# Where four table rows are summed: VectorE or accumulating transfers, in one stage of a two-layer macaron kernel

## The reference, cut to what matters

```python
x = x + 0.5 * _L0_ffn_ref(_layernorm(x), ...)   # 32 routed experts, top 4, plus a shared one
x = x + _L0_attn_ref(_layernorm(x), ...)        # gated linear attention
x = x + 0.5 * _L0_ffn_ref(_layernorm(x), ...)   # the routed experts again
x = x + 0.5 * _L1_ffn_ref(_layernorm(x), ...)   # 8 experts, top 2   <- the stage of the change
x = x + _L1_attn_ref(_layernorm(x), ...)        # token mixing with a scan
x = x + 0.5 * _L1_ffn_ref(_layernorm(x), ...)
```

## Time and profile before

| what | value |
|---|---|
| runs shown | 1115.69, 1108.85 and 1122.56 us, median 1115.69 |
| profiled execution | 1114.38 us, of which the span of the trace is 1112.5 us |
| granted TensorE clock, mean of the span | 0.94 |
| busy share of the span | TensorE 88%, VectorE 65%, ScalarE 50%, GpSimd 34% |
| stage ffn1a | 744.3 us (mark L1962) to 871.3 us, when the token mixing starts |
| stage ffn1b | 1015.4 us (mark) to 1112 us |

### The profile page before, as it was taken

One profiled execution on the slowest core, in us unless ns is written; L12 is line 12 of the kernel. 1 busy time (PEld: TensorE's weight loads), 2 busy tenths in 40 slices (PEclk: granted clock), 3 DMA queues, 4 the chain that ended last, 5 costly groups with the idle time before them and its releaser, 6 DMA issues. The chain is left out here.

```text
span 1112.5 us, 17325 instructions
## 1 busy us (share of the span) xinstructions
PE 980.2 (88%) x5222; PEld 602.2 (54%) x5240; DVE 720.9 (65%) x2533; ACT 551.0 (50%) x1066; POOL 378.6 (34%) x452
## 2 busy tenths in 40 slices
PE   6999699979999799998999898956778899994886
PEld 4756566645565366665756666532334466553442
DVE  4588333137885467665688533159987699974885
ACT  6621233325666645547722333326667555534893
POOL 3106767820000223323105777801111156531110
PEclk9999799998999699999999999987889899996998
DMA  9859978864440802004246888757420000000012
GB/s 326 322 179 316 161 201 228 156 171 152 152 151 0 319 32 95 38 38 143 79 160 123 188 199 189 134 185 240 152 75 1 1 0 1 0 1 0 21 57 76
DMA packets 79656, 140.73 MB, mean 126 GB/s; under 512 B 16304, under 2 KB 47392, under 8 KB 77472
## 3 DMA queue, kind: packets, MB, share of 16 engines
q1 hardware_dynamic: 64224, 117.57, 30.8%
q0 software_dynamic: 15360, 22.29, 13.3%
HBM read 82.17 MB, written 58.72 MB: 127 GB/s over the span
## 5 line engine op out<-in xcount | busy, mean ns | idle before, releaser
L737 POOL DMA_INDIRECT ffn_sums<-ffn0a_xT,ffn0a_into x40 | 62.7, 1567 | 19.9 <-issue 9.3
L737 POOL DMA_INDIRECT ffn_sums<-ffn0b_xT,ffn0b_into x40 | 62.6, 1564 | 14.7 <-issue 9.5
L2291 PE MATMUL main_ps_k<-dense_first_xb,main_w 128*128 128x512 bf16 x112 | 37.8, 410 | 17.5 <-ACT ffn1a_silu L2226 8.3
L2716 PE MATMUL main_ps_k<-mixing_first_xk,mixing_wk 128*128 128x512 f32 (+1 forms) x96 | 47.0, 613 | 4.2 <-POOL main_opened_mark L1962 4.2
L1768 POOL TENSOR_TENSOR attn_attend_state_m<-attn_attend_state,attn_attend_heads 128x512 f32<-128x512 f32 x15 | 19.1, 1274 | 88.4 <-DVE attn_attend_state L1811 82.9
L2721 PE MATMUL attn_ps_r<-mixing_first_xr,mixing_wr 128*128 128x512 f32 (+1 forms) x96 | 46.2, 605 | 0.0
L1193 DVE TENSOR_TENSOR ffn0b_h<-ffn0b_sg,ffn0b_ps_b 128x160 f32<-128x160 f32 x32 | 10.3, 321 | 54.9 <-ACT ffn0b_sg L1028 54.8
L1193 DVE TENSOR_TENSOR ffn0a_h<-ffn0a_sg,ffn0a_ps_b 128x160 f32<-128x160 f32 x32 | 10.3, 321 | 54.2 <-ACT ffn0a_sg L1028 54.1
L2731 PE MATMUL attn_ps_y<-mixing_wv,attn_out 128*128 128x256 f32 (+1 forms) x192 | 43.0, 379 | 1.2 <-ACT attn_yn L2673 1.2
L866 PE MATMUL ffn0b_ps_b<-ffn0b_early,main_x 128*128 128x160 f32 x256 | 41.3, 305 | 2.6 <-DMA main_x<-w_experts 2.3
L888 PE MATMUL ffn0a_ps_b<-main_x,ffn0a_h 128*32 128x256 f32 (+2 forms) x144 | 43.5, 403 | 0.0
(11 more groups left out here) (498 smaller groups left out, 2682.3 us busy)
## 6 DMA issues: line engine op xcount, KB each, us to landing
main_spare<-ffn_sums SPq DMA_DIRECT2D x28, 1024.0 KB, 5.4
main_x<-w_experts SPq DMA_DIRECT2D x16, 1536.0 KB, 7.0
ffn_sums<-main_lent SPq DMA_DIRECT2D x36, 512.0 KB, 6.0
ffn_sums<-main_x SPq DMA_DIRECT2D x28, 512.0 KB, 4.1
ffn_rows<-ffn0a_early SPq DMA_DIRECT2D x8, 512.0 KB, 9.3
main_spare<-ffn_sums SPq DMA_DIRECT2D x8, 512.0 KB, 4.7
ffn_rows<-ffn0b_early SPq DMA_DIRECT2D x8, 512.0 KB, 2.9
x_out<-main_x SPq DMA_DIRECT2D x8, 512.0 KB, 2.9
```

What stands on the lines that cost most here:

```text
L737: g.indirect_dma_start(out=sums[:, :], out_offset=IndirectOffsetOnAxis(ap=into[:, at, j:j + 1], axis=0), in_=ys[:, n % NY, :], in_offset=N ...
L2291: ins = mm(ps[:], wt[:, k, m * P:(m + 1) * P], xb[:, p, k, :], start=k == 0, stop=k == KD - 1)
L2716: ins = mm(ps_k[0:rows, m % 2], wk[:, k, at:at + rows], xk[:, p, k, :], start=k == 0, stop=k == KD - 1)
```

## The change

For blocks 4 to 7 VectorE no longer adds rows. SyncE loads table 0's rows of a block (512 KB) straight into x (`sp_base`); GpSimd then issues three transfers of 512 KB for each block, which add the rows of tables 1, 2 and 3 to x (`pool_sum`), each when the one before has landed in the same block. VectorE waits for the last of them (`dve_summed`) and takes the moments. Blocks 1 to 3 are summed as before.

```diff
+    def sp_base(self, b):
+        tiles = slice(b * BT, (b + 1) * BT)
+        self.nc.sync.dma_start(self.x[:, tiles, :], self.by_row[:, 0, tiles]).then_inc(self.base_landed[b - 4], 16)
+
+    def pool_sum(self, b, n):
+        g, tiles = self.nc.gpsimd, slice(b * BT, (b + 1) * BT)
+        if n == 1:
+            g.wait_ge(self.base_landed[b - 4], 16)
+        else:
+            g.wait_ge(self.part_summed[b - 4], 16 * (n - 1))
+        if n == NTAB - 1 and b >= 6:
+            g.wait_ge(self.x_summed[b % 2], 16 * (b // 2 - 2))
+        ins = g.dma_start(self.x[:, tiles, :], self.by_row[:, n, tiles], accum_op=ALU.add)
...
+    def dve_summed(self, j):
+        (b, p, i), v = j, self.nc.vector
+        v.wait_ge(self.x_summed[p], 16 * i - 16)
+        v.memset(self.waiter[:], 0.0)
...
                 if combine:
-                    for b in range(2, NB):
-                        combine.sp(b)
-                        if b == 3 and load_next:
-                            load_next()
+                    combine.sp(2)
+                    for b in range(4, 7):
+                        combine.sp_base(b)
+                    sp.wait_ge(xb_made, 1)
+                    combine.sp_base(7)
+                    combine.sp(3)
+                    if load_next:
+                        load_next()
...
-                each(pool, ln.pool, NB, 1 if combine else 2)
+                if combine:
+                    ln.pool(number(1))
+                    combine.pool_sum(4, 1)
+                    combine.pool_sum(5, 1)
+                    ln.pool(number(2))
+                    combine.pool_sum(4, 2)
+                    combine.pool_sum(5, 2)
+                    combine.pool_sum(6, 1)
+                    ln.pool(number(3))
+                    combine.pool_sum(4, 3)
+                    combine.pool_sum(5, 3)
+                    combine.pool_sum(6, 2)
+                    combine.pool_sum(7, 1)
+                    ln.pool(number(4))
+                    combine.pool_sum(6, 3)
+                    combine.pool_sum(7, 2)
+                    ln.pool(number(5))
+                    combine.pool_sum(7, 3)
+                    ln.pool(number(6))
+                    ln.pool(number(7))
...
-                        if m == 0 and j2 and combine:
+                        whole = combine and j2 and isinstance(j2[0], int)
+                        if m == 0 and whole:
                             combine.dve(j2, 0)
                         if m == 2 and j2:
-                            if combine:
+                            if whole:
                                 combine.dve(j2, 1)
+                            elif combine:
+                                combine.dve_summed(j2)
                             moments(j2)
```

More of the change, by code:

```diff
@@ L1316, in __init__, with into_x @@
         self.late_step = sc.sem(f"{name}_late_step")
+    def into_x(self, sc):
+        self.base_landed = [sc.sem(f"base_landed{b}") for b in range(4, NB)]
+        self.part_summed = [sc.sem(f"part_summed{b}") for b in range(4, NB)]
+        self.x_summed = [sc.sem(f"x_summed{p}") for p in range(2)]
+    def sp_base(self, b):
[10 more added lines that the diff above has]
+        ins = g.dma_start(self.x[:, tiles, :], self.by_row[:, n, tiles], accum_op=ALU.add)
+        if n < NTAB - 1:
+            ins.then_inc(self.part_summed[b - 4], 16)
+        else:
+            ins.then_inc(self.x_summed[b % 2], 16)
+    def dve_summed(self, j):
+        (b, p, i), v = j, self.nc.vector
+        v.wait_ge(self.x_summed[p], 16 * i - 16)
+        v.memset(self.waiter[:], 0.0)
     def sp_first(self, n):
@@ L2070, in ffn1 @@
         G_STEPS = 10
+        if combine:
+            combine.into_x(sc)
         def tile_of(j):
@@ L2093, in _ @@
                 opened.pool()
-                each(pool, ln.pool, NB, 1 if combine else 2)
+                if combine:
+                    ln.pool(number(1))
[17 more added lines that the diff above has]
+                    ln.pool(number(7))
+                else:
+                    each(pool, ln.pool, NB, 2)
                 if following:
```

## The result

With the change the kernel takes 1104.13 us (median of 17 runs, 1101.23 to 1109.07), against 1115.69 us for the kernel before (17 runs). The ratio is 0.9901, with a 95% interval of 0.9882 to 0.9919: faster by 1%, some 11 us. The forecast was 1108, the range 1097 to 1119. The profiled execution took 1103.4 us, with a span of 1101.5 us. It starts the stage at 747.08 us (before 744.26) and the token mixing at 860.23 us (before 871.21).

A forecast was written before the change was run, and what follows sets the result against it. VectorE was taken to bound rounds 2 to 5 of ffn1a (busy 51.2 of 54.6 us). 1114.4 - 14.0 (additions removed) + 5.0 (block 3) + 2.5 (block 4 and TensorE's clock) = 1107.9, stated as 1108; range 1097 to 1119.

The forecast's parts named there:

- What is removed: Rounds 2 to 5 of ffn1a: without VectorE's additions they shorten from 54.6 to ffn1b's 40.6 us, at most 14.0 us gained.
- Block 3: VectorE's first addition of block 3 waits for its load behind four 0.5 MB loads and beside sums: 5.0 us, ends 1.0 and 7.6.
- the 210 of the experts' weights: Block 3's half beside sums: load rate of 210 GB/s, from 1.5 MB in 7.5 us beside scattering additions; wait 4.8 us.
- The upper end: Wait at block 3 if its half shares the DMA engines equally with the first sums of blocks 4 and 5: 7.6 us.
- Block 4 and TensorE's clock: Rounds 2 to 5: wait for block 4's last sum and TensorE's lower clock, together 2.5 us, ends 0 and 6.6.
- The price of a sum: DMA engines' time for a 0.52 MB sum at the scattering additions' 144 GB/s: 3.6 us of all engines.
- the 1 to 2 us of GpSimd's time: On GpSimd: each of the 12 transfers should take 1 to 2 us to issue.
- The landing of 7.2 us: Block 4's third sum: lands 4.5 us plus 2.7 us after its issue, at 783.1 us.
- a sign of being wrong: Prediction is wrong if sums land later than 10 us after issue, block 3's wait is gone, or rounds do not shorten.
- rounds 6 to 9 do not change: Last four rounds of ffn1a: they hold no sum and do not change.
- All of it arrives: Rival: loads go at 350 GB/s, sums land in time, block 3 waits 1.0 us; 1101.4 us, chance 0.20.
- Given back inside the stage: Rival: block 3 waits 7.6 us and TensorE keeps today's clock in rounds 2 to 5 (6.6 us); 1114.6 us, chance 0.20.
- Slower: Rival: the twelve sums come one behind the other, 7.5 us each, block 7 ready at 849; 1137 us, chance 0.07.

The follow-up runs named there:

- the two pairs of profiles: Changed kernel and kernel before, each profiled once, then each run once more without any edit for a second profile: 1106.26 us and 1114.1 us.
- the one with the busier TensorE: Kernel before, with the first matmul of each of TensorE's eight group-opening products per round done twice in rounds 2 to 5 of ffn1a: 1116.59 us.
- both moves: Changed kernel, loads of blocks 6 and 7 behind block 3's, first sums of blocks 4 and 5 behind block 2's `ln.pool`, block 3's `ln.pool` moved ahead: 1108.76 us.
- plain copies: Changed kernel with GpSimd's twelve transfers as plain copies that overwrite x instead of adding to it: 1104.4 us, ratio 0.9905.
- the second and third experiments: Changed kernel, second: loads of blocks 6 and 7 behind block 3's halves, 1100.58 us; third: first sums of blocks 4 and 5 behind block 2's `ln.pool`, 1100.9 us.

## Why the prediction was right, and where it was not

**What is removed: right.** 14.0 us were forecast for rounds 2 to 5; the two pairs of profiles show 13.9 and 14.1. The argument, that ffn1b is the same code without the sums and so shows the floor, gave the length of these rounds to 0.1 us (40.6 and 40.7), and the additions put back on VectorE take it away again.

**Block 3: right in size, through two errors that cancel.** 5.0 us were forecast, with ends of 1.0 and 7.6; the waits are 4.62 and 3.74 us, the opening is longer by 4.7 and 3.1. Loads and sums sharing the engines was the assumed cause, and either taken away removes the wait. But they did not share as the sum has it. Here are the two DMA queues of the changed kernel, q1 with SyncE's loads and q0 with GpSimd's sums (packets, MB, share of all engines), first from 757.1 to 764.1 us, where q0 has moved almost nothing although the first sum was issued at 760.01, then from 764.1 to 771.1:

```profile
q1 hardware_dynamic: 977, 2.85, 102.7%
q0 software_dynamic: 1, 0.00, 0.5%
```

```profile
q0 software_dynamic: 284, 1.04, 75.0%
q1 hardware_dynamic: 362, 0.71, 30.1%
```

In the first stretch the loads go at 407 GB/s, where the sum took 269. By its end SyncE's queue has moved 5.00 MB since the stage opened; the loads up to and with block 3's first half are 5.24 MB. In the second the loads get 101 GB/s, where the sum took the 210 of the experts' weights beside scattering additions, and the half lands only at 771.2, when the first sum and nearly all of the second are done. Faster loads up to the sums and slower ones beside them came to about the forecast wait: that the size is right is luck. The upper end stood for an equal share of the DMA engines between the two queues. The Trainium skill ("DMA: Bandwidth & Descriptors", section Queues, rings and completion order) says that an engine takes its queues in turn, packet by packet. The trace is in keeping with that, 284 packets against 362, but not with equal time: one of a sum took 0.30 us of an engine on average and one of a load 0.09 (share x 7 us x 16 engines / packets).

**Block 4 and TensorE's clock: mis-sized.** 2.5 us were put down for both, and measured is nothing: the memset has no wait, and TensorE has 0.98 in rounds 2 to 5. The sum itself came as forecast: issued 36.3 us behind the mark (783.41 - 747.08; forecast 775.82 + 5.0 - 744.26 = 36.6) and landed 5.5 us later, at 788.9, where the sum had 7.2 (it makes 783.1 of 775.82 + 7.2, which is 783.0). VectorE got there at 789.85. It is a narrow escape: with the loads in the other order the same memset waits 0.60 us. The price of a sum was well bounded: 144 GB/s were assumed, 160 measured alone; the 1 to 2 us of GpSimd's time came out at 0.9. The landing of 7.2 us lies between the 5.6 alone and the 8.2 in company. Three of the twelve landed later than 10 us after their issue (10.7, 11.4 and 11.5), which the prediction had named as a sign of being wrong; VectorE waited for none of them. The Trainium skill's fit for a transfer that GpSimd issues ("DMA: Bandwidth & Descriptors", Anatomy of one DMA: about 2.0 us plus the bytes at 436 GB/s, by which this size is estimated at 3.2 us) is too low for both kinds here, by 0.7 us for the plain copy and 2.4 for the addition.

**What the sum left out.** It said that rounds 6 to 9 do not change. They are shorter by 4.6 and 2.0 us in the two pairs. Everywhere in the table their length goes with the granted clock: 36.9 us at 0.99 and 1.00, 38.1 at 0.96, 38.7 to 39.6 at 0.90 and 0.91, 41.5 at 0.83, with VectorE's and ScalarE's work unchanged. Part of this belongs to the change. Round 6 takes 9.4 us in all six profiles without VectorE's additions in the loop and 10.1 to 12.1 in the four with them, and putting the additions back takes it from 9.4 to 12.1. The last 5 us before round 6 and its first 10 us, for the changed kernel, the kernel before, the one with the additions again and the one with the busier TensorE:

```profile
818.31:823.31 5.00, 3.98 (x38) 2.17 (x38) 4.82 (x23) 4.34 (x9) 1.37 (x3) 1.00 0.00 0
823.31:833.31 10.00, 8.76 (x65) 4.71 (x66) 8.13 (x44) 9.06 (x20) 0.39 (x5) 1.00 0.00 0
```

```profile
824.71:829.71 5.00, 2.18 (x9) 0.71 (x9) 4.77 (x16) 1.76 (x4) 1.37 (x3) 0.96 0.00 0
829.71:839.71 10.00, 9.72 (x56) 5.44 (x58) 7.04 (x35) 7.43 (x15) 0.39 (x5) 0.68 0.00 0
```

```profile
826.21:831.21 5.00, 2.47 (x10) 0.80 (x10) 4.92 (x16) 1.76 (x4) 1.37 (x3) 1.00 0.00 0
831.21:841.21 10.00, 9.30 (x52) 4.74 (x53) 6.66 (x34) 7.24 (x14) 0.38 (x5) 0.66 0.00 0
```

```profile
824.18:829.18 5.00, 2.76 (x12) 0.91 (x11) 4.77 (x16) 1.76 (x4) 1.37 (x3) 1.00 0.00 0
829.18:839.18 10.00, 9.52 (x61) 4.96 (x61) 7.51 (x35) 8.23 (x18) 0.39 (x5) 0.83 0.01 2
```

Where VectorE adds, TensorE is busy for only 2.18 to 2.76 of the last 5 us (3.98 in the changed kernel), and the clock falls as round 6 begins (0.66 to 0.83 over 10 us, 1.00 in the changed kernel). That the additions cost the clock there is shown by the kernel that puts them back; that TensorE's standing still is the way is argued, since the matmuls done twice did not fill that place. Round 6 makes 2.0 of the 4.6 us and 0.7 of the 2.0. The rest comes from low clock later in the four rounds, which kernels without the additions have too (39.4 us with both moves, 38.1 with plain copies); whether the change has a part in it stays open.

Ahead of the stage there is a difference the other way: the marks of the changed kernel's profiles stand at 747.08 and 749.71 us, those of the kernel before at 744.26 and 744.64 (plain copies 748.92, all others 742.79 to 745.60). Part of it is a lower clock near the program's start, from 58 to 70 us, the kernel before first:

```profile
58.00:70.00 12.00, 11.17 (x45) 6.70 (x45) 10.42 (x78) 1.99 (x5) 0.00 (x0) 1.00 0.22 86
```

```profile
58.00:70.00 12.00, 11.17 (x39) 6.02 (x39) 9.39 (x63) 2.52 (x4) 0.00 (x0) 0.88 0.23 91
```

Behind this stretch the changed kernel is 1.8 and 1.7 us late in its two profiles, and the one with plain copies 1.6 us (ScalarE's next activation, L996, starts at 75.08, 74.92 and 74.80 us); in the others it starts at 73.13 to 73.34. That code is the same in all of them. Why it happens stays open, and so does how much of the 2.5 us by which the second and third experiments seem better comes from there.

**The balance.** For the first pair: 2.8 (ahead of the stage) + 4.7 - 13.9 - 4.6 + 0.0 (behind it) = -11.0 us of span. For the second pair: 5.1 + 3.1 - 14.1 - 2.0 + 0.1 = -7.8. The medians say -11.6. The forecast was -6.5. The first pair gained 4.5 us more: 2.5 that did not come, 4.6 in the last rounds and 0.2 in the two large terms, less the 2.8 ahead of the stage. The second gained 1.3 more, and that it is so close is luck: the 5.1 us ahead of the stage stand against 2.5, 2.0 and the 1.9 by which the opening grew less than forecast.

**The rivals.** "All of it arrives" named a time (1101.4) nearer to the 1104.13 measured than the forecast is, and the loads did go fast and the sums did land in time; but its wait of 1.0 us was 4.62 and 3.74, since the sums met the last of the load. "Given back inside the stage" did not happen in the changed kernel. "Slower" needed 5.6 us or more from sum to sum; the twelve took 50.1 us from the first issue (760.01) to the last landing (804.53 + 5.6), 4.2 us each. Its mechanism is real all the same: in the kernel with both moves late sums hold up `ln.pool`, and ScalarE with it.

## What to carry to other kernels

Where the same code runs elsewhere without the work in question, its rows are the best estimate of what removing that work is worth, and of who is next. What an in-order queue with dependent transfers does to the rest is decided by what stands behind each wait: a chain of accumulating transfers is cheap on the issuing engine, but each wait for the one before holds back every small step behind it, so put these steps ahead of any wait that may not be over. Take a second profile before explaining a stretch that the change does not touch: of 4.6 us here 2.6 lay between two executions of one kernel. And check each term of a sum by itself: a total, or a wait, that comes out as forecast can hide errors that cancel.

## What the runs showed of the hardware

An accumulating transfer of 0.5 MB into SBUF keeps all DMA engines busy for 3.3 us, a plain one of the same shape from the same engine for 1.9 us; alone they land after 5.6 and 3.9 us, and in company the medians are 8.2 and 6.0. GpSimd needs 0.91 us to issue the one and 0.56 for the other, both less than the 1.55 us of the scattering additions from which the prediction priced them. Block 3's half of 1 MB landed 5.4 us after its issue in the kernel before, and 13.8 us beside two of these sums and behind 2 MB of other loads. While loads and sums both moved, the sums' packets took 75% of the engines' time and the loads' 30%, and the loads fell from 407 to 101 GB/s.
